# Source one-hots of the edge network made two pairs ahead and set between the products and the low parts

## The reference, cut to what matters

```python
W_e = (e @ W_enet + b_enet).reshape(-1, in_dim, out_dim)
msg = jnp.einsum('ei,eio->eo', v[src], W_e)
agg_sum = jax.ops.segment_sum(msg, tgt, num_segments=N)
agg = agg_sum / jnp.maximum(cnt, 1.0)[:, None]
h = agg + v @ W_root + bias
# batch norm over the nodes, leaky relu, + v
```

## Time and profile before

| what | value |
|---|---|
| median of 3 runs | 4043.86 us (4042.63 to 4044.53) |
| the profiled execution | 4042.56 us, of which the span from first to last instruction 4041.0 us |
| PE (TensorE matmul) busy | 3445.0 us (85%) |
| DVE (VectorE) busy | 3339.0 us (83%) |
| ACT (ScalarE) busy | 2651.9 us (66%) |
| POOL (GpSimd) busy | 2793.7 us (69%) |
| granted TensorE clock, mean | 0.934 of full speed |

### The profile page before, as it was taken

How to read it: one execution, slowest core, us unless ns; L and a number is a source line. 1 busy time by engine, 2 the same in 40 slices (tenths; PEclk the granted TensorE clock), 3 DMA queues, 4 the chain that set the end, 5 groups by cost and what they waited for, 6 DMA issues and landing times.

```text
span 4041.0 us, 105133 instructions
## 1 busy us (share of the span) xinstructions
PE 3445.0 (85%) x28550; PEld 2890.6 (72%) x28556; DVE 3339.0 (83%) x6551; ACT 2651.9 (66%) x3636; POOL 2793.7 (69%) x2751
## 2 busy tenths in 40 slices
PE   3459999999999699999999977778776898878887
PEld 3438888888888577777777766777775777757775
DVE  6789999999999688888888887888886887768876
ACT  2149999999999599999999970000003566646665
POOL 4447777777777377777777747776653777657774
PEclk9989999999999799999999998777777999989998
DMA  6011111111111321111111111111111222222221
GB/s 80 27 16 24 24 25 25 24 24 24 26 24 24 24 29 31 29 31 31 31 29 31 31 23 30 30 28 27 24 20 24 44 44 41 40 34 45 43 42 28
DMA packets 285654, 124.21 MB, mean 31 GB/s; under 512 B 179726, under 2 KB 260338, under 8 KB 285622
## 3 DMA queue, kind: packets, MB, share of 16 engines
q1 hardware_dynamic: 186838, 87.92, 9.6%
q0 software_dynamic: 84672, 29.47, 8.6%
q10 hardware_dynamic: 14112, 6.43, 0.7%
HBM read 121.80 MB, written 1.78 MB: 31 GB/s over the span
## 4 chain that ended last, share of the span: by engine, by line
PE 33%; issue 21%; POOL 20%; DVE 15%; DVEq 5%; DMA 3%; ACT 1%; POOLq 0%; SPq 0%; ACTq 0%
POOL gb L448 17%; PE ps L719 10%; PE ps L735 10%; PE ps L839 6%; POOL gb L438 3%; PE ps L725 2%; DVE oht L1301 2%; PE ps L855 2%; DVEq L286 2%; DVE oh L970 2%; PE ps L633 1%; DVE oht L1370 1%; DVE rest L986 1%; DMA eat<-vtab 1%; DVE xt L1106 1%
## 5 line engine op out<-in xcount | busy, mean ns | idle before, releaser
L448 POOL DMA_INDIRECT gb<-table,idx x1568 | 1618.5, 1032 | 565.9 <-issue 451.1
L438 POOL DMA_INDIRECT gb<-table,idx x1078 | 1084.7, 1006 | 541.1 <-issue 449.3
L719 PE MATMUL ps<-big,oh 128*128 128x290 f32 (+1 forms) x7840 | 1266.1, 308 | 1.6 <-DVE big L1146 1.6
L719 PEld LDWEIGHTS ps<-big,oh 128*128 128x128 f32 x7840 | 1071.1, 191 | 124.8 <-DVE big L1146 2.2
L735 PE MATMUL ps<-w,ht 128*128 128x320 f32 x3136 | 1008.4, 444 | 119.9 <-DVE xt L1106 107.5
L548 ACT ACTIVATE oh<-iota_f,src_n 128x640 fp32r<-128x640 f32 x1372 | 1024.6, 815 | 0.0
L551 ACT ACTIVATE oh<-oh,ones 128x2560 fp32r<-128x2560 f32 (+1 forms) x392 | 849.6, 2167 | 12.8
L735 PEld LDWEIGHTS ps<-w,ht 128*128 128x128 f32 x3136 | 556.8, 191 | 381.0 <-DVE xt L1106 177.6
L1106 DVE TENSOR_TENSOR xt<-ps,gb 128x640 f32<-128x640 f32 x784 | 642.1, 819 | 76.6 <-PE ps L735 25.1
L599 ACT ACTIVATE rest<-rest,dst_f x1220 | 383.0, 389 | 320.6 <-PE ps L855 277.1
L1114 DVE TENSOR_REDUCE msg<-xt 128x80 f32<-128x1280 f32 (+1 forms) x392 | 580.1, 1480 | 0.0
(11 more groups left out here) (223 smaller groups left out, 2828.3 us busy)
## 6 DMA issues: line engine op xcount, KB each, us to landing
gb<-table,idx POOLq DMA_INDIRECT x2646, 2.4
eat<-in_eat SPq DMA_DIRECT2D x196, 192.0 KB, 2.4
eat<-vtab SPq DMA_DIRECT2D x98, 160.0 KB
eat<-vtab SPq DMA_DIRECT2D x49, 256.0 KB
eat<-vtab SPq DMA_DIRECT2D x98, 128.0 KB
rest<-in_edge_attr ACTq DMA_DIRECT2D x98, 64.0 KB, 1.9
idx<-in_src SPq DMA_DIRECT2D x245, 4.0 KB
idx<-in_dst SPq DMA_DIRECT2D x196, 4.0 KB
```

The costliest lines, as they stand in the source:

```text
L438: nc.gpsimd.indirect_dma_start(out=(gb if p == 2 else gr)[:, b, t, 0:tabw[p]], out_offset=None, in_=tabs[p], in_offset=bass.IndirectOffset ...
L448: nc.gpsimd.indirect_dma_start(out=gb[:, b, t, 0:tabw[p]], out_offset=None, in_=tabs[p], in_offset=bass.IndirectOffsetOnAxis(ap=idx[:, b, ...
L719: mm = nc.tensor.matmul(out, oh5[:, b, t, c * P:(c + 1) * P], big[:, b, t, 0:W], start=False, stop=False, skip_group_check=True)
```

## The change

VectorE's step(j) no longer begins with the source one-hots of pair j + 1. It makes those of pair j + 2, of the same parity k and so into the same buffers, between the products and the low parts of the second tile. Behind them, and also ahead of the low parts, it reads the block word of pair j, which `pair_onehots` read itself before. The one-hots of pairs 0 and 1 are made ahead of the loop, and the loop has one round less, with its last round written out, since the last two steps have no pair to look ahead to. `pair_onehots` is used by the edge network alone. No other engine's program changes.

```diff
--- before.py
+++ after.py
@@ -960,8 +960,8 @@
             def one_sup(ap3, s):
                 return ap3[:, bass.ds(s, 1), :].rearrange("p o t -> p (o t)")
 
-            def pair_onehots(w, j):
-                lo, hi, off = load_window(dve, j, win2)
+            def pair_onehots(w, j, bounds):
+                lo, hi, off = bounds
                 with dve.Fori(lo, hi) as c:
                     c = nc.s_assert_within(c, 0, NB - 1, skip_runtime_bounds_check_because="a block index out of the window table")
                     for h in range(2):
@@ -1339,8 +1339,6 @@
 
                 def step(j, i, k, ahead):
                     s = i * 4 + 2 * k
-                    if ahead:
-                        source_onehots(j + 1, i + k, 1 - k)
                     dve.wait_ge(g_in[2][k], (i + 1) * 16 * T)
                     edge_products(s, 0, gb[:, k, :, 0:D])
                     select_rows(j, k, 0)
@@ -1348,13 +1346,19 @@
                     select_rows(j, k, 1)
                     dve.wait_ge(rd_done, j * 2 + 5)
                     edge_products(s + 1, 1, gx[:, k, :, :])
+                    if ahead:
+                        source_onehots(j + 2, i + 1, k)
+                    bounds = load_window(dve, j, win2)
                     low_parts(s + 1, 1)
-                    pair_onehots(1, j)
-
-                source_onehots(0, 0, 0)
-                with dve.Fori(0, QUADS) as i:
+                    pair_onehots(1, j, bounds)
+
+                for k in range(2):
+                    source_onehots(k, 0, k)
+                with dve.Fori(0, QUADS - 1) as i:
                     for k in range(2):
                         step(i * 2 + k, i, k, True)
+                step(PAIRS - 3, QUADS - 1, 0, True)
+                step(PAIRS - 2, QUADS - 1, 1, False)
                 step(PAIRS - 1, QUADS, 0, False)
 
             def tile_onehots(p, s, b, n, first):
```

## The result

| kernel | median | lowest to highest | runs | ratio to before (95%) |
|---|---|---|---|---|
| before, measured beside it | 4043.24 us | 4039.69 to 4044.53 | 4 | |
| after | 4088.87 us | 4083.96 to 4094.30 | 4 | 1.0113 (1.0101 to 1.0125) |

The account below looks back on a forecast made before the run. No engine is full; VectorE's own order sets the pace. Gains 9.8 + 12.1 + 1.3 + 1.9 - 0.9 = 24.2 us; 4042.6 - 24.2 + 1.3 = 4019.7 us, range 4010 to 4028.

Parts of the forecast that it names:

- GpSimd at 11.1 keeps up: Edge-network gathers, pairs 22 to 46: at 11.1 us a pair GpSimd keeps up with VectorE's mean period.
- 11.4 as a rival: GpSimd slowed to 11.4 us a pair by meeting more VectorE work: 7 us of gain lost, 4026; chance 0.12.
- the sum: The edge network's predicted gain, added up over groups of pairs: 24.2 us.
- the shared ports' rule: SBUF ports: whichever VectorE two-port or GpSimd instruction starts first blocks the other; one-hots showed at most 0.17 us over median.
- the first nine pairs: Opening stretch of one-window pairs, GpSimd only 0.83 us ahead: held by gathers, they win no more than 0.8 us.
- The new wait behind double pairs: VectorE idle before first low parts, for ScalarE and TensorE's closing matmul: about 1.4 us after pairs with two windows.
- No ScalarE wait before the second low parts and no issue time before L970: Signs of being right: VectorE's idle times of 37.7 us before low parts and 36.6 us before window one-hots go.
- The block word: Read early: low parts to window one-hots 0.5 us instead of 1.31; rival, it stays on the path, 4042, chance 0.05.
- The clock rivals: TensorE at full clock longer, 11 us more gain, 0.14; or clock falling before windows, 0.11 in part, 0.08 in full.
- the slower of the two: Clock falls before TensorE's windows: 12 us lost, 4032, chance 0.11 in part; 45 us, 4065, 0.08 in full.
- Row copies straight behind the windows: Sign of being right: TensorE's row copies follow its windows at once, without the 1.33 us wait for VectorE.
- Pair 22: Edge network: pair 22 starts at 2676.5 in the timeline, where it was 2686.33, a gain of 9.8 us.

Follow-up runs that it names:

- e3: After, with VectorE waiting for its own low parts before the window one-hots, ahead of the loop's set-up: 4051.04 us, ratio 1.0017.
- e5: After, with VectorE waiting for its own low parts inside the window loop, right before the first window one-hot: 4032.84 us, ratio 0.9972.
- e2: Before, with only the block word's read moved ahead of the second tile's low parts: 4029.86 us, ratio 0.9964.
- e15: The kernel of e2 (before, only the block word's read moved) again on another chip: 4031.03 us, ratio 0.9968.
- e4: After, with a wait between the two one-hots of each window, the second waiting for the first: 4053.28 us, ratio 1.0017.
- e1: After, with the block word read behind the low parts again: 4095.64 us, ratio 1.012.
- e12: After, with three of the five source one-hots put at the next step's start; head one-hot, two others and word's read stay: 4008.92 us, ratio 0.9913.
- e13: After, with the fifth source one-hot put between low parts and window one-hots, no wait added: 4034.52 us, ratio 0.9976.
- e6: After, with only four of the eight gathers of each edge-network pair: 4008.89 us, ratio 0.9914.
- e7: Before, with only four of the eight gathers of each edge-network pair: 4039.15 us, ratio 0.9986.
- e8: e5 plus eight matmuls on zeros between TensorE's row copies and its windows: 4030.72 us, ratio 0.9966.

## Why the prediction was wrong, point by point

**The step that failed is "GpSimd at 11.1 keeps up".** Its rate had been taken from before and held to be a property of GpSimd (11.4 as a rival, because it "meets more VectorE work"). It was the rate of gathers beside a VectorE queue that had a break ahead of L970 in every pair, and the change removed that break. At 13.1 us a pair GpSimd is slower than the 10.85 to 11.1 of before by some 2 us, and that is the price that the sum lacked: 49 pairs at 13.1 are 642 of the stage's 651 us, where the forecast came to 577. The rival had the sign and the engine right, but not the size (0.3 instead of 2) nor the mechanism, and it was priced for the pairs where it would bind, when it binds in 46 of the 48 behind the first.

A table makes the mechanism plain. The spacing is from the start of the low parts to the start of the first window one-hot, in the first 47 pairs:

| kernel | spacing, us | gather started under the low parts or the window one-hots |
|---|---|---|
| before | 1.29 to 1.38 | at most 1.69 us |
| e3 | 1.10 to 1.17 | at most 1.97 |
| e5 | 0.73 to 0.77 | at most 1.66 |
| e2, e15 | 0.56 to 0.61 | at most 1.85 |
| e4 (break one instruction later) | 0.46 and 0.47 | mostly 2.39 and 2.8, none longer |
| after, e1 | 0.46 and 0.47 | 3.1 to 3.9, mostly 3.53, in 46 of 47 pairs |

That an unbroken run of VectorE's instructions can shut the gather out, and that a break lets it in, is shown by e3, e4 and e5: only a break was added, and the gather's end followed it. That an unbroken run always does so is wrong. In before, e2, e3 and e5 the two window one-hots follow each other without a break, and in 45 to 47 of the first 47 pairs a gather that begins under the first of them is let in behind it. There the run was broken ahead of the first. Even that is not needed in e12. Twelve of its pairs have 0.46 or 0.47 as well, and 2.34 or 2.35 for the two window one-hots as in after; yet in eleven of them the gather that begins 0.73 us into the first ends 0.8 behind that one, after 1.3 us. The twelfth has a twin in after, with the gather's start 0.03 to 0.04 us into the first window one-hot in both, and ends in 2.00 us where the twin takes 3.13 (e12, then after, where the low parts start at 2608.30):

```profile
2965.20 2.35 DVE L970 TENSOR_TENSOR oh<-dst_f,iota_f 128x1024 fp32r<-128x1024 f32 x2
2965.23 2.00 POOL L438 DMA_INDIRECT gb<-table,idx  x1 [0.30 <-issue]
```

```profile
2608.80 3.13 POOL L438 DMA_INDIRECT gb<-table,idx  x1 [0.30 <-issue]
```

In e13 one that begins 0.81 into it ends 0.82 behind the second, after 2.36. So which seam between two queued instructions is open is decided by something finer than the hundredths of the trace. A queue that is full against one filled just in time would fit, but is only argued, and stays open.

**A rule read for one side only.** The prediction held the shared ports' rule against the one-hots' durations alone. The rule names two losers. On VectorE's side L1301 shows next to nothing: it takes 482 ns on average in after, 480 in before. But another line, the f32 copy at L1316, shows it in before already. 26 of its 98 copies take 0.32 to 0.35 us instead of 0.22. Each begins 0.65 us or more into a gather and ends 0.05 us behind the gather's end:

```profile
2472.17 0.95 POOL L438 DMA_INDIRECT gb<-table,idx  x1 [0.30 <-issue]
...
2472.82 0.34 DVE L1316 COPY v<-gb 128x128 f32<-128x128 f32 x1
```

In after 20 copies take up to 0.46. In all that is 2.9 us in before and 3.5 in after, so it decides nothing; but the prediction's "the trace does not bear it out for VectorE" was read off the wrong line. On GpSimd's side the trace has it at 3.53 us. The Trainium skill (SBUF — State Buffer, A bandwidth-pool intuition that's wrong) tells of just this, a transfer from GpSimd's queue that takes five times as long because its descriptors have to wait for VectorE's instruction to end. The traces agree with the blocking and differ in two things. The wait goes over a run of up to three instructions and not one, and the transfer ends 0.82 us after them. And the blocking instructions are f32 tensor_tensor ones with two SBUF inputs (L1321, L970). Of these the same page (Who interferes with whom) says that they contend with a GpSimd instruction that reads SBUF, and infers that they don't stall the writing of descriptors. The gathers here read their indices from SBUF (idx), so the first sentence may be what is seen; no run has a transfer without indices beside them. Against the inference alone, the measurement decides.

**VectorE's sum was right in kind and near in size.** The gain without GpSimd in the way is 30.3 us (e6 against e7). The 24.2 of the sum still had the first nine pairs held by GpSimd; without that hold it would be up to 40, as was written ahead of e6. e5, with everything moved and the gathers healed, gained 11.5 us and paid 9.4 for its break, together 20.9. The new wait behind double pairs, taken as 1.4 us, is 0.5 to 1.8 in e6, with a median of 1.5. No ScalarE wait before the second low parts and no issue time before L970 came as written, and after's own 12 waits before L1321 are few (e6 has 37) because a VectorE held up by gathers gives TensorE time.

**The block word** was right: e1 shows that its read is hidden anywhere behind the one-hots, and e2 and e15 price it alone at 13 to 15 us. So two thirds of e5's 20.9 come from one line. With the break that the long gathers call for, moving all of the one-hots adds nothing over it (4032.84 against 4029.86 and 4031.03). The move itself is worth more, about half of the 30.3 us, but part of what the block wins behind the products it gives back in front of the next ones; e12 keeps both.

**The clock rivals** do not explain the loss. TensorE's window matmuls take 303 ns on average in after and 312 in before (1168 of them), and e8's clock of 0.82 brought 2 us. But after cannot test the slower of the two, since its VectorE waits for gathers. Where it doesn't, these matmuls do get slower, 331 ns in e6 and 326 in e5, though the granted clock of the stretch to 3000 us is 0.79 and 0.78. That is the sign of the rival; what it costs there is not measured, and the 30.3 us of e6 have it in them. **Row copies straight behind the windows** did not come: the copy at 2499.30 waited 3.61 us for VectorE, which itself waited for the gather. **Pair 22** was to start near 2676; in after it starts at 2721.45, and in e12 at 2675.52.

## What to carry to other kernels

Before moving work so that VectorE's instructions join up, look at what GpSimd issues beside them. The rate of its indirect transfers need not be its own: here it fell from eight in 11.0 us to eight in 13.1 when the breaks in VectorE's queue went. The longest single transfer, next to the VectorE run around it, shows it sooner than any mean. If a stall is filled with independent work, put there only as much as the stall needs; two of the five one-hots here, with the word's read, won three times what all of them did with it and a break behind (34.7 us against 11.5).

## What the runs showed of the hardware that had not been expected

- A gather by indirect transfer that takes 0.94 us alone takes 3.1 to 3.9 in after when it starts just ahead of or under an unbroken run of three f32 two-input VectorE instructions. It ends 0.81 to 0.83 us behind the point where it is let in, in before, after, e2 and e4 alike.
- In e2 a tenth of a microsecond more between the starts (0.57 against 0.47 us), which leaves 0.01 us between the two instructions, goes with the gather let in. In e13 long and short gathers go with spacings a hundredth apart.
- The other way round, an f32 copy of VectorE that begins late in a gather ends only 0.05 us behind it, 0.32 to 0.46 us long instead of 0.22 (before, after).
- The f16 to bf16 one-hots with one input (L1301), just as dense, stretch a gather only to 0.97 to 1.32 us in after. They are also shorter, 0.48 us against 1.22.
- Waiting for one's own last instruction costs 0.19 us if the wait stands right at the next instruction (e5) and 0.58 if the loop's set-up has to follow it (e3).
- One chip ran the same kernel in 5187 us where the others take 4043. What is different there was not looked into.
